# An RWKV-6 mixer with a ternary feed-forward: a fifth product in split form, two moved reductions, and one diagonal copy changed from GpSimd to ScalarE

## The chip, the cores and the metric

One core of a Trainium2 chip runs the program. The metric is device time in microseconds for one launch, the median of several runs. The times name the engines as the profile does: PE is TensorE (its weight loads stand apart as PEld), DVE is VectorE, ACT is ScalarE, POOL is GpSimd, SP is SyncE, which here only issues DMAs.

## What is computed

One layer over x of shape 4 x 2048 x 512 (batch, time, channels), with two residual blocks and a layer normalisation after each:

```python
xx = x_prev - x
mix = tanh((x + xx * time_maa_x) @ maa_w1).reshape(b, t, 5, 32)
mw, mk, mv, mr, mg = einsum('btfe,fec->fbtc', mix, maa_w2)
xk = x + xx * (time_maa_k + mk)          # the same for w, v, r, g
r = xr @ Wr.T;  k = xk @ Wk.T;  v = xv @ Wv.T;  g = silu(xg @ Wg.T)
w = time_decay + tanh(xw @ td_w1) @ td_w2;  decay = exp(-exp(w))
# 16 heads of 32: y_t = r_t (S + u k_t v_t),  S = decay_t S + k_t v_t
y = groupnorm(y) * ln_g + ln_b;  att = (y * g) @ Wo.T
x = layernorm(x + att)
h = gelu(x @ ternary(W_fc).T)
x = layernorm(x + layernorm(h, ln_w, ln_b) @ ternary(W_proj).T)
```

Everything is fp32 at the outside. `mg`, the fifth of the mixing products, is one part of the change.

## The kernel before

The sequence is cut into 32 chunks of 64 steps. A *tile* is one chunk of all four sequences, so 256 columns (`COLS`), with the 512 channels as four groups of 128 partitions. Each engine has a program of its own: `tile(it, first, ffn)` is the attention part of chunk `it`, and between its pieces it calls pieces of the feed-forward of chunk `it - 1` (and a last piece of `it - 2`). Chunks 0 and 1 and the last feed-forward are written out, chunks 2 to 31 are a loop (`over_tiles`). No scheduler is at work: the order on an engine is the order of the code, and engines meet at counting semaphores. PSUM banks go round in rings (`P_SEQ`, `M_SEQ`, `W_SEQ`, `X_SEQ`, `F_SEQ`), each entry with the engine that empties it.

What the change touches, in the order of a tile:

- **The mixing products** (`mix` on PE, L380). ACT takes the tanh of 128 rows for w, k, v, r (`TMA`, L795) and of 32 rows for g (`TMB`, L797). For the first four, the 32 rows of a factor are written four times, one above another, into a 128-row tile `MT[f]`: two copies rounded to the reduced-precision fp32 format (high part, by ACT in `mix_high`, L666), two of what the rounding left (low part, by POOL in `mix_low`, L869). The weights `W2S` are stacked to match (split in setup, L858 and L860), so that one 128-row product of reduced-precision operands gives all four cross terms. The fifth, g, is a plain fp32 product of 32 rows, `W2B` by `TMB`. Each product is four matmuls of 128x256, in two PSUM banks (psX, psY), read by DVE in L1064.
- **The levels.** The recurrence inside a chunk is done by halves: `LEVELS = (2, 4, 8, 16)` and then 32. On each level DVE scales the right halves of the queries (`scale_right`, L1119, with a copy L1107), scales the left halves of the keys (`scale_left`, L1131, and the totals L1132), and takes the level's product from PSUM (L1174). ACT makes three copies of queries for each level (L666), PE the product (L469, for 32 it is L486), followed by a quarter of the down projection of the feed-forward (L642).
- **The folds.** DVE sums GELU values and their squares over the 2048 hidden channels (`add`, L1279 and L1282), and folds four columns of each into one: `fold(p, i)`, L1298, a reduction of 128x512 to 128x128, i = 0 for the values, 1 for the squares. PE multiplies both with ones (`stats`, L632) right after L486. Before the change, for the first half of the tokens, they stand after the levels 4 and 8:

```python
                    dve.wait_ge(w_dve, W.read(it, f"l{n}"))
                    if ffn and n in (4, 8):
                        ffn.fold(0, n // 4 - 1)
                scale(5, 32)
```

- **The diagonal copies.** The 16 x 32 x 32 blocks of the finished matrix `A` are copied onto the diagonal of `AB`, by row groups q = 0 to 3. For the second half (p = 1) ACT makes q = 0 and 1 in `matrices(1)` (L666), then two more copies from PSUM; POOL makes q = 2 and 3 (L909). PE's `from_chunk(1)` (L523) waits for both. ACT then goes on with `squares(0)` (L774), the GELU group `up(1, 0)` (L814, L823, L825), `squares(1)`, and `up(1, 1)`.
- **The end of a tile.** POOL makes the eight low parts, then takes the inverse root of the variance (L876), after which DVE normalises (L1263); in the next tile POOL adds x to the mixed inputs (L883).

Of the kernel before, what the change touches and what calls it, by code (L numbers as in the profile page):

```python
# [104 lines left out]
def rwkv_ffn_kernel(nc, x_ch, x_tok, w_all, w1, w2a, w2b, td1, td2, par, wfc, wpj, ffn_wb, c_f32, c_mask, out,  # L105
                    tiles=TILES):
    with ExitStack() as ctx:
# [39 lines left out]
        TMH = K1[:, 0:COLS]  # L147
# [12 lines left out]
        TMA = sb("TMA", [128, COLS])  # L160
        MTALL = sb("MT", [128, 4, COLS], F32R)
        MT = [MTALL[:, f, :] for f in range(4)]
        TZTM = sb("TZTM", [DECR + MIXR, COLS])
        TZ, TMB = TZTM[0:DECR, :], TZTM[DECR:DECR + MIXR, :]
# [32 lines left out]
        W2RAW = (OUT[:, 0:2, :], X1[:, 0:2, :])  # L197
# [67 lines left out]
        NWEIGHTS = 8 + 4 * 4  # L265
# [15 lines left out]
        def _(sp):  # L281
# [8 lines left out]
            for dst, src in ((W1[:, :, :], w1), (W2B[:, :], w2b), (TD1[:, :, :], td1),  # L290
                             (TD2[:, :], td2), (WALL[:, W_K, :, :], w_all[:, W_K, :, :])):
                sp.dma_start(dst, src).then_inc(weights_in, 16)
            for f in range(4):
                for copy in range(4):
                    sp.dma_start(W2RAW[f // 2][rows(copy), f % 2, :], w2a[rows(f), :]).then_inc(weights_in, 16)
# [35 lines left out]
        def _(pe):  # L331
# [37 lines left out]
            def mix(t, f, name, wait_free):  # L369

                if f < 4:
                    pe.wait_ge(mt_high, 4 * (t + 1) + f + 1)
                    pe.wait_ge(mt_low, 8 * (t + 1) + 2 * f + 2)
                else:
                    pe.wait_ge(tm_ready, M.read(t, "w1b"))
                lhs, rhs = (W2S[:, f, :], MT[f]) if f < 4 else (W2B[:, :], TMB[:, :])
                for g in range(2):
                    wait_free(f"{name}{g}")
                    for c in range(2):
                        mm = pe.matmul(M_BANKS[M.bank(f"{name}{g}")][:, COLS * c:COLS * (c + 1)],  # L380
                                       lhs[:, 128 * (2 * g + c):128 * (2 * g + c + 1)], rhs, start=True, stop=True)
# [282 lines left out]
        def _(act):  # L664
# [3 lines left out]
            def mix_high(t):  # L668

                act.wait_ge(tm_ready, M.read(t, "w1a"))  # L670
                copy(TMH.bitcast(F32R), TMA[:, :]).then_inc(tm_rounded, 1)
                for f in range(4):
# [12 lines left out]
            def tile(it, first, ffn):  # L685
# [21 lines left out]
                act.wait_ge(mt_low, 8 * (it + 1))  # L707
# [46 lines left out]
                def matrices(p):  # L754
# [5 lines left out]
                    for q in range(2 if p else 4):  # L760
# [33 lines left out]
                act.wait_ge(mt_low, 8 * (it + 1))  # L794
# [42 lines left out]
        def _(pool):  # L837
# [24 lines left out]
            def mix_low(t):  # L862

                pool.wait_ge(tm_rounded, t + 2)
                for n in range(8):
                    if n:
                        pool.wait_ge(mt_low, 8 * (t + 1) + n)
                    f = n // 2
                    pool.tensor_tensor(MT[f][rows(1 + 2 * (n % 2)), :], TMA[rows(f), :], TMH[rows(f), :], ALU.subtract).then_inc(mt_low, 1)  # L869
                pool.wait_ge(mt_low, 8 * (t + 1) + 8)  # L870

            pool.wait_ge(w2_split, 4)
# [5 lines left out]
            def tile(it, first, ffn):  # L878
# [93 lines left out]
        def _(dve):  # L972
# [111 lines left out]
            def tile(it, first, ffn):  # L1084
# [80 lines left out]
                for i, n in enumerate(LEVELS):  # L1165
# [52 lines left out]
                dve.wait_ge(ab_rest, 2 * it + 2)  # L1218
# [209 lines left out]
```

## Time and profile before

| | |
|---|---|
| median of 3 runs | 3344.99 us (3342.59 to 3347.0) |
| the profiled execution: its own time, its span | 3343.92 us, 3342.1 us |
| mean granted TensorE clock | 0.993 |
| busy: PE, PEld, DVE, ACT, POOL | 3093.1, 2244.0, 2437.3, 1858.8, 962.3 us |
| chain that ended last, by engine | PE 48%, DVE 31%, issue 11%, ACT 8% |

The table is read from the bottom up: the busy times say how much work each engine has, but the chain says whose work the end waited for. PE is busy 93% of the span and yet only 48% of the chain: in the rest of a tile it has work, or a short wait, while something else is late.

### The profile page before, as it was taken

How to read it: one execution, taken by the hardware profiler on the slowest of the kernel's cores; microseconds unless marked ns; L12 is line 12 of the kernel's file. 1: busy time of each engine (PE TensorE's matmuls, PEld its weight loads, DVE VectorE, ACT ScalarE, POOL GpSimd, SP SyncE). 2: the span in 40 equal slices, each digit the busy share in tenths (PEclk: the TensorE clock that was granted, in tenths of full speed). 3: DMA queues.
4: the chain of work that ended last, by engine and by line, in shares of the span. 5: the costliest groups of instructions: out<-in, count | busy, mean ns of one | idle time of the engine just before them, and what ended most of it. 6: DMA issues, size and time to landing. Idle time of an engine off the chain costs nothing.

```text
span 3342.1 us, 99122 instructions
## 1 busy us (share of the span) xinstructions
PE 3093.1 (93%) x39261; PEld 2244.0 (67%) x39261; DVE 2437.3 (73%) x5172; ACT 1858.8 (56%) x3788; POOL 962.3 (29%) x789
## 2 busy tenths in 40 slices
PE   1899999999999999999999999999999999999997
PEld 0667666767666767666767666767666767666765
DVE  8467787777787777687777687777687677687777
ACT  0445566555566555566655566655566655556654
POOL 4223322223322223322223322223322223322232
PEclk9899999999999999999999999999999999999999
DMA  5000000000000000000000000000000000000000
GB/s 193 14 8 21 15 18 21 18 14 21 15 18 21 18 14 21 18 14 21 18 14 21 21 12 21 18 14 21 21 12 21 18 16 19 21 12 21 18 19 16
DMA packets 22597, 73.04 MB, mean 22 GB/s; under 512 B 3040, under 2 KB 3296, under 8 KB 20544
## 3 DMA queue, kind: packets, MB, share of 16 engines
q1 hardware_dynamic: 22208, 66.76, 5.8%
q8 instruction: 378, 6.19, 0.8%
q14 instruction: 11, 0.09, 0.0%
HBM read 49.97 MB, written 16.78 MB: 20 GB/s over the span
## 4 chain that ended last, share of the span: by engine, by line
PE 48%; DVE 31%; issue 11%; ACT 8%; DVEq 1%; DMA 1%; POOL 0%; ACTq 0%; SPq 0%; POOLq 0%
PE psP L398 11%; PE psF L623 7%; PE psP L430 7%; PE psP L596 5%; DVE ARENA L1131 4%; ACT HHI L823 4%; DVE HLO L1290 4%; DVE ARENA L1174 3%; DVE ARENA L1143 3%; DVE ARENA L1119 3%; DVE SUMS L1282 2%; PE psX L380 2%; ACT GG L814 2%; PE psY L523 2%; PE psY L511 2%
## 5 line engine op out<-in xcount | busy, mean ns | idle before, releaser
L398 PE MATMUL psP<-ARENA,WALL 128*128 128x256 f32 x3072 | 690.9, 382 | 0.2 <-ACT ARENA L697 0.2
L666 ACT ACTIVATE ARENA<-ARENA 32x512 f32<-32x512 f32 (+1 forms) x928 | 537.9, 580 | 252.8 <-DVE ARENA L1119 224.5
L398 PEld LDWEIGHTS psP<-ARENA,WALL 128*128 128x128 f32 x3072 | 574.4, 190 | 83.4 <-issue 11.3
L1290 DVE SCALAR_TENSOR_TENSOR HLO<-GG,FWB,HHI 128x128 f16<-128x128 f32 x1024 | 302.5, 357 | 370.7 <-ACT HHI L823 364.3
L623 PE MATMUL psF<-XHI,WFC 128*128 128x128 f16 x4096 | 488.3, 220 | 2.4 <-DVE ST L1308 2.1
L623 PE MATMUL psF<-XLO,WFC 128*128 128x128 f16 x4096 | 487.1, 220 | 0.0
L883 POOL TENSOR_TENSOR ARENA<-ARENA,XT 128x1024 f32<-128x1024 f32 x128 | 278.4, 2175 | 546.8 <-DVE ARENA L1064 546.8
L623 PEld LDWEIGHTS psF<-XHI,WFC 128*128 128x128 f16 x4096 | 400.7, 99 | 31.5 <-issue 26.2
L623 PEld LDWEIGHTS psF<-XLO,WFC 128*128 128x128 f16 x4096 | 402.1, 98 | 17.6 <-issue 10.3
L642 PE MATMUL psF<-WPJ,HHI 128*128 128x512 f16 x1024 | 390.9, 382 | 3.8 <-ACT GG L814 3.8
L642 PE MATMUL psF<-WPJ,HLO 128*128 128x512 f16 x1024 | 389.4, 380 | 0.0
L823 ACT ACTIVATE HHI<-GG,FWB 128x128 f16<-128x128 f32 x1024 | 327.4, 390 | 25.3
L876 POOL TENSOR_TENSOR FV<-FV,CF 128x1 f32<-128x1 f32 x64 | 43.1, 674 | 1035.7 <-DVE FV L1314 1035.7
L1064 DVE SCALAR_TENSOR_TENSOR ARENA<-psX,PAR,XX 128x256 f32<-128x256 f32 x322 | 140.2, 476 | 235.8 <-PE psX L380 216.3
L814 ACT ACTIVATE GG<-psF 128x512 f32<-128x512 f32 x256 | 152.4, 595 | 280.4 <-PE psP L398 185.3
L869 POOL TENSOR_TENSOR MT<-TMA,ARENA 32x256 fp32r<-32x256 f32 x264 | 258.7, 980 | 95.2 <-ACT ARENA L666 77.1
L596 PE MATMUL psP<-WALL,ARENA 128*128 128x512 f32 x512 | 233.4, 599 | 2.8 <-DVE ARENA L1233 0.2
L430 PE MATMUL psP<-WALL,ARENA 128*128 128x512 f32 x512 | 224.9, 592 | 0.0
L469 PE MATMUL psW<-ARENA 128*32 128x64 f32 x8192 | 142.5, 222 | 66.0 <-ACT ARENA L666 59.2
L469 PEld LDWEIGHTS psW<-ARENA 128*32 128x32 f32 x8192 | 121.9, 111 | 120.8 <-ACT ARENA L666 88.8
L642 PEld LDWEIGHTS psF<-WPJ,HHI 128*128 128x128 f16 x1024 | 100.1, 98 | 126.3 <-issue 16.4
L666 ACT ACTIVATE ARENA<-psP 128x256 f32<-128x256 f32 (+1 forms) x192 | 93.5, 525 | 154.1 <-PE psP L398 154.1
(167 smaller groups left out, 5398.8 us busy)
## 6 DMA issues: line engine op xcount, KB each, us to landing
XT<-x_ch SPq DMA_DIRECT2D x33, 520.0 KB, 3.4
ARENA<-x_tok SPq DMA_DIRECT2D x32, 512.0 KB, 3.8
out<-OUT SPq DMA_DIRECT2D x64, 256.0 KB, 2.1
WALL<-w_all SPq DMA_DIRECT2D x5, 1024.0 KB, 16.7
ARENA<-wfc SPq DMA_DIRECT2D x4, 1024.0 KB, 8.0
ARENA<-wpj SPq DMA_DIRECT2D x3, 1024.0 KB, 14.8
GG<-wpj SPq DMA_DIRECT2D x1, 1024.0 KB, 18.7
OUT<-w2a SPq DMA_DIRECT2D x8, 64.0 KB, 14.8
```

The costliest lines, as they stand in the source:

```text
L398: mm = pe.matmul(psP[:, P.bank(f"{name}{g}"), COLS * c:COLS * (c + 1)], WALL[:, w, k, 128 * (2 * g + c):128 * (2 * g + c + 1)], cc(XF[slot ...
L430: mm = pe.matmul(psP[:, P.bank(f"v{p}"), :], cc(XF[1], k)[:, 128 * p:128 * (p + 1)], WALL[:, W_V, k, :], start=(k == 0), stop=(k == KC - 1))
L469: mm = pe.matmul(psW[BLK * (q % 4):BLK * (q % 4 + 1), W.bank(name), o:o + 64], cc(KM, c)[:, BLK * q:BLK * (q + 1)], RB[RB_SEQ[name]][:, c, ...
L596: mm = pe.matmul(psP[:, P.bank(f"wo{p}"), :], cc(YSB, k)[:, 128 * p:128 * (p + 1)], WALL[:, W_O, k, :], start=(k == 0), stop=(k == KC - 1))
L623: mm = pe.matmul(psF[:, F.bank(name), 128 * m:128 * (m + 1)], WFC[:, k, 128 * (4 * g + m):128 * (4 * g + m + 1)], x[:, p, k, :], start=(k ...
L642: mm = pe.matmul(psF[:, F.bank(f"pj_{p}"), :], h[:, m, :], WPJ[:, m, :], start=(m == 0 and h is HHI), stop=(m == MH - 1 and h is HLO))
L666: return act.activation(o, i, ACT.Copy)
L814: act.activation(GG[:, u % 2, 0, :], psF[:, F.bank(f"fc{g}_{p}"), :], ACT.Gelu).then_inc(f_act, 1)
L823: e = act.activation(HHI[:, k, :], GG[:, u % 2, 0, 128 * m:128 * (m + 1)], ACT.Copy, scale=FWB[:, 0, k:k + 1])
L869: pool.tensor_tensor(MT[f][rows(1 + 2 * (n % 2)), :], TMA[rows(f), :], TMH[rows(f), :], ALU.subtract).then_inc(mt_low, 1)
L883: pool.tensor_tensor(v, v, xcur, ALU.add).then_inc(xf_ready, 1)
L1290: e = dve.scalar_tensor_tensor(out=HLO[:, k, :], in0=GG[:, u % 2, 0, 128 * m:128 * (m + 1)], scalar=FWB[:, 0, k:k + 1], in1=HHI[:, k, :], ...
```

## The change

It has three parts.

1. `mg` is made as the other four: a fifth slot in `W2S` and in `MT`, two more rounded copies on ACT per tile and one of `TMB` itself (`TMBH`), two more low parts on POOL. `TMA`, `TMH`, `TMB` and `TMBH` now lie in the four quarters of `K1`. In setup, four DMAs bring the weights of g into `V` in place of one, and POOL has one more cast and one more subtraction.
2. `fold(0, 0)` stands after level 2, and `fold(0, 1)` between `scale_right(5, 32)` and `scale_left(5, 32)`.
3. For p = 1, ACT copies q = 0, 1, 2 and POOL only q = 3.

```diff
             def mix(t, f, name, wait_free):
-                if f < 4:
-                    pe.wait_ge(mt_high, 4 * (t + 1) + f + 1)
-                    pe.wait_ge(mt_low, 8 * (t + 1) + 2 * f + 2)
-                else:
-                    pe.wait_ge(tm_ready, M.read(t, "w1b"))
-                lhs, rhs = (W2S[:, f, :], MT[f]) if f < 4 else (W2B[:, :], TMB[:, :])
+                pe.wait_ge(mt_high, 5 * (t + 1) + f + 1)
+                pe.wait_ge(mt_low, 10 * (t + 1) + 2 * f + 2)
+                lhs, rhs = W2S[:, f, :], MT[f]
...
             def mix_high(t):
-                act.wait_ge(tm_ready, M.read(t, "w1a"))
+                act.wait_ge(tm_ready, M.read(t, "w1b"))
                 copy(TMH.bitcast(F32R), TMA[:, :]).then_inc(tm_rounded, 1)
-                for f in range(4):
-                    copy(MT[f][rows(0), :], TMA[rows(f), :])
-                    copy(MT[f][rows(2), :], TMA[rows(f), :]).then_inc(mt_high, 1)
+                copy(TMBH.bitcast(F32R), TMB[:, :]).then_inc(tm_rounded, 1)
+                for f in range(5):
+                    src = TMA[rows(f), :] if f < 4 else TMB
+                    copy(MT[f][rows(0), :], src)
+                    copy(MT[f][rows(2), :], src).then_inc(mt_high, 1)
...
-                    for q in range(2 if p else 4):
+                    for q in range(3 if p else 4):
...
             def mix_low(t):
-                pool.wait_ge(tm_rounded, t + 2)
-                for n in range(8):
+                pool.wait_ge(tm_rounded, 2 * t + 4)
+                for n in range(10):
...
-                for q in range(2, 4):
-                    if q == 3:
-                        pool.wait_ge(ab_rest, 2 * it + 1)
-                    r = slice(BLK * q, BLK * (q + 1))
-                    block = A[r, 512:1024].rearrange("p (h t) -> p h t", h=HEADS)
-                    pool.tensor_tensor(AB[r, :, BLK * q:BLK * (q + 1)], block, ONES[r, 0:BLK].unsqueeze(1).broadcast_to([BLK, HEADS, BLK]), ALU.mult).then_inc(ab_rest, 1)
-                pool.wait_ge(ab_rest, 2 * it + 2)
+                r = slice(BLK * 3, BLK * 4)
+                pool.tensor_tensor(AB[r, :, BLK * 3:BLK * 4], A[r, 512:1024].rearrange("p (h t) -> p h t", h=HEADS),
+                                   ONES[r, 0:BLK].unsqueeze(1).broadcast_to([BLK, HEADS, BLK]), ALU.mult).then_inc(ab_rest, 1)
+                pool.wait_ge(ab_rest, it + 1)
...
                     dve.wait_ge(w_dve, W.read(it, f"l{n}"))
-                    if ffn and n in (4, 8):
-                        ffn.fold(0, n // 4 - 1)
-                scale(5, 32)
+                    if ffn and n == 2:
+                        ffn.fold(0, 0)
+                scale_right(5, 32)
+                if ffn:
+                    ffn.fold(0, 1)
+                scale_left(5, 32)
```

The order of instructions, at three places. DVE in the levels of a tile before the change; GR<-SUMS is a fold, ARENA<-CM,psW the taking of a level's product (128x128x4 is level 4, 128x64x8 level 8):

```order
L1174 COPY_PREDICATED ARENA<-CM,psW 128x128x4
L1298 TENSOR_REDUCE GR<-SUMS 128x128
L1119 TENSOR_TENSOR ARENA<-ARENA,TOT 128x64x8
L1107 COPY ARENA<-ARENA 32x4x128
L1131 TENSOR_TENSOR ARENA<-ARENA,TOT 128x64x8
L1132 TENSOR_TENSOR TOT<-TOT 128x64
L975 MEMSET PAUSE 1x1
L1174 COPY_PREDICATED ARENA<-CM,psW 128x64x8
L1298 TENSOR_REDUCE GR<-SUMS 128x128
L1119 TENSOR_TENSOR ARENA<-ARENA,TOT 128x32x16
```

DVE in the changed kernel, from the taking of level 2's product on:

```order
L1169 COPY_PREDICATED ARENA<-CM,psW 128x256x2
L1296 TENSOR_REDUCE GR<-SUMS 128x128
L1114 TENSOR_TENSOR ARENA<-ARENA,TOT 128x128x4
L1102 COPY ARENA<-ARENA 32x4x128
L1126 TENSOR_TENSOR ARENA<-ARENA,TOT 128x128x4
```

The first fold has moved one level forward. DVE in the changed kernel, from the taking of level 16's product on:

```order
L1169 COPY_PREDICATED ARENA<-CM,psW 128x32x16
L1114 TENSOR_TENSOR ARENA<-ARENA,TOT 128x16x32
L1296 TENSOR_REDUCE GR<-SUMS 128x128
L1126 TENSOR_TENSOR ARENA<-ARENA,TOT 128x16x32
L1127 TENSOR_TENSOR TOT<-TOT 128x16
```

The second fold has moved behind the level 16 and stands between the two scalings of level 32; no fold is left between levels 4 and 16. ACT from the copies out of psX (the transposed keys) to the GELU group after, before the change:

```order
L666 ACTIVATE ARENA<-psX 128x512 x2
L666 ACTIVATE ARENA<-ARENA 32x16x32 x2
L666 ACTIVATE ARENA<-psW 32x16x32 x2
L774 ACTIVATE ARENA<-ARENA 128x4x128
L814 ACTIVATE GG<-psF 128x512
```

and in the changed kernel:

```order
L661 ACTIVATE ARENA<-psX 128x512 x2
L661 ACTIVATE ARENA<-ARENA 32x16x32 x3
L661 ACTIVATE ARENA<-psW 32x16x32 x2
L771 ACTIVATE ARENA<-ARENA 128x4x128
L811 ACTIVATE GG<-psF 128x512
```

One more diagonal copy stands ahead of the copies from psW, which PE waits for, and ahead of the GELU group.

## Rows read from the trace of the kernel before

**Rows 1.** The page: busy times, and the chain by engine.
```profile
PE 3093.1 (93%) x39261; PEld 2244.0 (67%) x39261; DVE 2437.3 (73%) x5172; ACT 1858.8 (56%) x3788; POOL 962.3 (29%) x789
PE 48%; DVE 31%; issue 11%; ACT 8%; DVEq 1%; DMA 1%; POOL 0%; ACTq 0%; SPq 0%; POOLq 0%
```

**Rows 2.** By tile: count, duration min/median/max ns, first and last start us.
```profile
L797 ACT ACTIVATE TZTM<-psY x32: 371/371/373, 179.7 to 3280.4; 32x256 f32<-32x256 f32 x32
L869 POOL TENSOR_TENSOR MT<-TMA,ARENA x264: 713/726/1947, 91.1 to 3288.1; 32x256 fp32r<-32x256 f32 x132
```

**Rows 3.** The chain of waits, 1700 to 1810: start us, us, what.
```profile
1713.27 1.05 PE psX L380 x4
...
1715.19 3.67 PE psP L398 x16
...
1719.03 0.61 ACT GG L814
...
1804.06 0.29 PE psX L380 x2
...
1804.58 5.58 PE psP L430 x13
```

**Rows 4.** Timeline of DVE: start us, us, what, [idle before <-releaser].
```profile
1744.78 0.69 DVE L1174 COPY_PREDICATED ARENA<-CM,psW 128x512 f32<-128x512 uint32 x1
...
1745.51 1.08 DVE L1298 TENSOR_REDUCE GR<-SUMS 128x128 f32<-128x512 f32 x1
1746.52 0.67 DVE L1119 TENSOR_TENSOR ARENA<-ARENA,TOT 128x512 f32<-128x512 f32 x1
...
1748.53 0.72 DVE L1174 COPY_PREDICATED ARENA<-CM,psW 128x512 f32<-128x512 uint32 x1
1749.44 0.69 DVE L1119 TENSOR_TENSOR ARENA<-ARENA,TOT 128x512 f32<-128x512 f32 x1 [0.19 <-DVE ARENA L1174]
1751.32 0.69 DVE L1131 TENSOR_TENSOR ARENA<-ARENA,TOT 128x512 f32<-128x512 f32 x1 [1.19 <-PE psW L486]
...
1792.74 1.83 DVE L1263 TENSOR_SCALAR X<-X,MV,RSTD 128x512 f32<-128x512 f32 x2
```

**Rows 5.** Timeline of PE.
```profile
1745.50 1.10 PE L469 MATMUL psW<-ARENA 128*32 128x64 f32 x64 [1.05 <-ACT ARENA L666]
...
1748.05 0.38 PE L642 MATMUL psF<-WPJ,HLO 128*128 128x512 f16 x1
1749.33 1.94 PE L486 MATMUL psW<-ARENA 128*32 128x128 f32 x32 [0.90 <-DVE ARENA L1174]
...
1759.15 1.08 PE L523 MATMUL psY<-ARENA,V 128*32 128x128 f32 x32 [0.85 <-issue]
```

**Rows 6.** Timeline of ACT.
```profile
1743.54 1.91 ACT L666 ACTIVATE ARENA<-ARENA 32x512 f32<-32x512 f32 x3 [2.08 <-DVE ARENA L1119]
...
1755.44 1.27 ACT L666 ACTIVATE ARENA<-ARENA 32x512 f32<-32x512 f32 x2 [0.44 <-PE psY L523]
1756.74 1.19 ACT L666 ACTIVATE ARENA<-psW 32x512 f32<-32x512 f32 x2
...
1761.02 0.62 ACT L774 ACTIVATE ARENA<-ARENA 128x512 f32<-128x512 f32 x1
1762.16 0.60 ACT L814 ACTIVATE GG<-psF 128x512 f32<-128x512 f32 x1 [0.52 <-PE psF L623]
```

**Rows 7.** Timeline of POOL: setup, then a tile.
```profile
91.07 6.30 POOL L869 TENSOR_TENSOR MT<-TMA,ARENA 32x256 fp32r<-32x256 f32 x8 [8.03 <-ACT ARENA L666]
...
1755.58 3.47 POOL L909 TENSOR_TENSOR ARENA<-ARENA,CF 32x512 f32<-32x512 f32 x2 [1.86 <-PE psY L523]
...
1779.75 8.51 POOL L869 TENSOR_TENSOR MT<-TMA,ARENA 32x256 fp32r<-32x256 f32 x8 [2.10 <-ACT ARENA L666]
1789.56 0.70 POOL L876 TENSOR_TENSOR RSTD<-RSTD,CF 128x2 f32<-128x2 f32 x1 [1.30 <-DVE RSTD L1255]
1791.65 2.18 POOL L883 TENSOR_TENSOR ARENA<-ARENA,XT 128x1024 f32<-128x1024 f32 x1 [1.39 <-DVE ARENA L1064]
```

More of the change, by code:

```diff
@@ L146, in rwkv_ffn_kernel @@
         K1 = ARENA1[:, 7168:8192]
-        TMH = K1[:, 0:COLS]
+        TMA, TMH = K1[:, 0:COLS], K1[:, COLS:2 * COLS]
+        TMB, TMBH = K1[0:MIXR, 2 * COLS:3 * COLS], K1[0:MIXR, 3 * COLS:4 * COLS]
         KT = ARENA1[:, 7168:8192].rearrange("p (q n) -> p q n", q=PAIRS)
@@ L159, in rwkv_ffn_kernel @@
         XX = sb("XX", [128, KC * B, CH])
[L160 to L164, printed above, removed]
+        MTALL = sb("MT", [128, 5, COLS], F32R)
+        MT = [MTALL[:, f, :] for f in range(5)]
+        TZ = sb("TZ", [DECR, COLS])[:, :]
         TOT = {1: D}
@@ L264, in rwkv_ffn_kernel @@
         NPL = len(LEVELS) + 2
[L265 removed]
+        NWEIGHTS = 7 + 5 * 4
         POOL_PARTS = (2, 5, 7)
@@ L289, in _ @@
             sp.dma_start(WALL[:, W_V, :, :], w_all[:, W_V, :, :]).then_inc(values_in, 16)
-            for dst, src in ((W1[:, :, :], w1), (W2B[:, :], w2b), (TD1[:, :, :], td1),
+            for dst, src in ((W1[:, :, :], w1), (TD1[:, :, :], td1),
                              (TD2[:, :], td2), (WALL[:, W_K, :, :], w_all[:, W_K, :, :])):
                 sp.dma_start(dst, src).then_inc(weights_in, 16)
-            for f in range(4):
+            for f in range(5):
                 for copy in range(4):
-                    sp.dma_start(W2RAW[f // 2][rows(copy), f % 2, :], w2a[rows(f), :]).then_inc(weights_in, 16)
+                    sp.dma_start(W2RAW[f // 2][rows(copy), f % 2, :], w2a[rows(f), :] if f < 4 else w2b).then_inc(weights_in, 16)
             for w in (W_R, W_G, W_O):
@@ L668, in mix_high @@
             def mix_high(t):
-                act.wait_ge(tm_ready, M.read(t, "w1a"))
+                act.wait_ge(tm_ready, M.read(t, "w1b"))
                 copy(TMH.bitcast(F32R), TMA[:, :]).then_inc(tm_rounded, 1)
-                for f in range(4):
-                    copy(MT[f][rows(0), :], TMA[rows(f), :])
-                    copy(MT[f][rows(2), :], TMA[rows(f), :]).then_inc(mt_high, 1)
+                copy(TMBH.bitcast(F32R), TMB[:, :]).then_inc(tm_rounded, 1)
+                for f in range(5):
+                    src = TMA[rows(f), :] if f < 4 else TMB
+                    copy(MT[f][rows(0), :], src)
+                    copy(MT[f][rows(2), :], src).then_inc(mt_high, 1)
             act.wait_ge(su_dve, 6)
@@ L853, in _ @@
             pool.wait_ge(weights_in, 16 * NWEIGHTS)
-            for i in range(2):
+            for i in range(3):
                 if i:
-                    pool.wait_ge(w2_split, 2)
-                w = W2S[:, 2 * i:2 * (i + 1), :]
+                    pool.wait_ge(w2_split, 2 * i)
+                w = W2S[:, 2 * i:min(2 * i + 2, 5), :]
                 pool.tensor_copy(w, W2RAW[i]).then_inc(w2_split, 1)
@@ L862, in mix_low @@
             def mix_low(t):
-                pool.wait_ge(tm_rounded, t + 2)
-                for n in range(8):
+                pool.wait_ge(tm_rounded, 2 * t + 4)
+                for n in range(10):
                     if n:
-                        pool.wait_ge(mt_low, 8 * (t + 1) + n)
+                        pool.wait_ge(mt_low, 10 * (t + 1) + n)
                     f = n // 2
-                    pool.tensor_tensor(MT[f][rows(1 + 2 * (n % 2)), :], TMA[rows(f), :], TMH[rows(f), :], ALU.subtract).then_inc(mt_low, 1)
-                pool.wait_ge(mt_low, 8 * (t + 1) + 8)
-            pool.wait_ge(w2_split, 4)
+                    whole, high = (TMA[rows(f), :], TMH[rows(f), :]) if f < 4 else (TMB, TMBH)
+                    pool.tensor_tensor(MT[f][rows(1 + 2 * (n % 2)), :], whole, high, ALU.subtract).then_inc(mt_low, 1)
+                pool.wait_ge(mt_low, 10 * (t + 1) + 10)
+            pool.wait_ge(w2_split, 6)
             mix_low(-1)
```

19 lines of the change are left out of this document (9 added, 10 removed).

## The prediction

> **What bounds the kernel now.** I read the page first. PE is busy 93% of the span, but makes only 48% of the chain that ended last, and DVE 31% [rows 1]. So no engine bounds it alone: inside each tile the lead changes hands, and a saving counts only where its engine leads. The second view, by tile, gives the period: the tanh of L797 starts 32 times, from 179.7 to 3280.4 us [rows 2], so 31 periods take 3100.7 us, 100.02 us each. Setup and end take the other 7% of the span and are hardly touched, so the question is what one period loses. The third view, the chain in order of time over one period in the middle, says who leads; the timelines of the engines say how much slack the others have. Four stretches of it matter:
>
> - 1711 to 1719: PE leads. The product of g stands on the chain, and ACT's GELU (L814) waits for the first r product behind it [rows 3].
> - 1721 to 1749: DVE leads, through the levels. The folds lie in it: the fold of level 8 starts as soon as the product is taken and the next scaling right behind it [rows 4].
> - 1749 to 1762: PE leads, with one wait of 0.85 us before L523 [rows 5]. The view calls it "issue", but by the code PE waits there for POOL's diagonal copies, and those end at 1755.58 + 3.47 = 1759.05 [rows 7].
> - from 1762.16 on ACT leads with the GELU groups. It had been idle for only 0.52 us before that [rows 6].
>
> **The g product.** Removed: four fp32 matmuls, from 1713.27 to the start of the r product at 1715.19, so 1.92 us. Added: four matmuls in the split form. The v product of the same shape and form takes from 1804.06 to 1804.58, so 0.52 us [rows 3]. Difference 1.40 us per tile, all of it on the chain, since ACT waits for PE behind it and DVE's levels wait for ACT; everything up to the levels moves with it. 32 tiles: **-44.8 us**. The new waits of that product (ten low parts, five high ones) end at about 1790 us of the tile, 20 us before PE comes to it: nothing. Bounds: 0 if the new form ran like the old, 1.92 if it were free; the row of the same form is nearest, so 1.40. The Trainium skill says (FP8 and Floating Point Precision, TensorE Precision Notes) that a true fp32 product takes four passes through the array. By that estimate three quarters of 1.92 go, 1.44, and the sum would be 1.3 us lower; no row shows passes.
>
> Its price elsewhere: ACT makes one more rounded copy ahead and two behind, at a place where PE leads with the output projection: nothing. POOL's first piece waits for one copy more, about 0.4 us. The eight pieces take 6.30 us in setup and 8.51 us in the tile [rows 7], with pieces between 0.71 and 1.95 us [rows 2]: in the tile, pieces stand and wait beside DVE, the first among them, so a later start of 0.4 us is mostly swallowed. Two more pieces, 0.80 us each (6.30 / 8), end at 1788.26 + 1.6 = 1789.86. Behind them in POOL's queue stands the root, which waited 1.30 us for DVE anyway [rows 7]; it comes 0.3 us late, and DVE uses it at 1792.74 only [rows 4], 2.2 us after its new end. The next addition, at 1791.65 [rows 7], finds POOL free by 1.1 us. So nothing per tile, but in the last tile, where no other work is there, the root is on the path: +0.3 us. If this cover were gone, 1.6 us per tile would show. In setup POOL is idle for 8.03 us before its low parts [rows 7]; one more cast and subtraction fit into that, as they are half the size of those before. Three more small DMAs land long before POOL asks. Setup: 0.
>
> **The folds.** Before, from the end of the taken product of level 8, 1744.78 + 0.69 = 1745.47, to the next scaling at 1746.52 are 1.05 us. Without a fold, after level 16, it is 1749.44 - 1749.25 = 0.19 us [rows 4]. So a fold costs the chain of levels 0.86 us. `fold(0, 0)` pays this after level 2 instead of level 4: no change at the start of level 8. `fold(0, 1)` leaves the levels: -0.86 us, if nobody else is then late. ACT's three copies for level 16's product end at 1743.54 + 1.91 = 1745.45 [rows 6], and the scaling that waits for them would start at 1745.66: 0.2 us to spare. PE's product at 1745.50 ends at 1746.60, and DVE's left scaling, which waits for it, would come at about 1746.8: also 0.2. Then L486: before it PE waited 0.90 us for DVE, with the down projection done at 1748.43 [rows 5]. Now DVE ends at 1748.39 and PE is late next, by nothing: -0.86 us is about all there was. In its new place the fold starts behind the right scaling and fills the 1.19 us in which DVE waited for L486 [rows 4]; it needs 1.05, so 0.1 us remain. The sums that it makes are needed by PE only after L486. 31 tiles have a feed-forward in them: **-26.7 us**. Bounds: 0 to 0.90 us per tile; if both slacks are 0.2 us less than I think, 0.5 is left.
>
> **The diagonal copy.** POOL's 3.47 us shrink to one copy, some 1.3 to 2.1 us, and end by 1757.7. ACT's two copies of 1.27 us become three, +0.635, so the copies from psW, which PE needs too, end at 1757.93 + 0.635 = 1758.57 [rows 6]. PE starts L523 at about 1758.6 instead of 1759.15: 0.55 us early. But behind it ACT becomes the late one: its work up to the GELU group at 1762.16 is contiguous but for 0.52 us, and 0.635 more is added. The chain from there on loses 0.115 us per tile: **+3.6 us**. What PE gains is spent waiting. Bounds: -0.55 if PE still led, +0.635 if there were no slack at all; the row with the 0.52 is the direct one.
>
> **Sum.** -44.8 - 26.7 + 3.6 + 0.3 = -67.6 us. The profiled execution took 3343.92, so 3276.3; it lies 1.07 under the median of the runs, so I forecast **3277 us**, 2.0% less. About 0.2%, 7 us, is what a measurement of this kernel can tell from no change. The forecast's own range is 3270 to 3290.
>
> **The rivals.**
>
> - *The fold's gain is lost* (0.09). Level 8's product on PE now comes 0.9 us later relative to the down projection, since its queries are scaled behind the first fold; if that pushed the next level's product, or ACT's copies were 0.9 us late, DVE would wait where it now folds. Against it: the two slacks above are positive. Then 3277 + 26.7 = 3304.
> - *PE keeps the lead after L523* (0.08), because ACT has more slack than one period shows. Then the copy gains 0.55 instead of losing 0.115: 31 x 0.665 = 20.6, and 3256.
> - *The g product does not get faster* (0.04), for instance by weight loads that do not hide behind such short matmuls. But the v, r, k and w products are the same instructions. 3277 + 44.8 = 3322.
> - *POOL and DVE hold each other: slower* (0.03). Pieces beside DVE took up to 1.95 us [rows 2]. If all ten of a tile did, with gaps of 0.08, they would end 20.3 us after 1779.75, at 1800.0; the root and the addition behind them may start no later than 1790.95. The excess of 9.1 us, less the 2.15 saved, would add 6.95 us to 31 tiles: 3345 + 215 = 3560. It decides from an end at 1793.1 on, that is at 1.33 us per piece with its gap, where the eight now take 1.06. Against it: all eight together lose 2.21 us to setup's 6.30 [rows 7], and where the two new ones fall, after 1788.3, DVE has by the code small statistics and reads from PSUM. The Trainium skill (SBUF — State Buffer, SBUF: two separate sides) has VectorE and GpSimd take one shared port pair as an exclusive lock: whoever starts first keeps it for the whole instruction, the other blocks. The 6.30 against 8.51 us agrees with it.
> - *Nothing measurable comes out* (0.02): gains in the first part of a tile are given back at its end, where DVE normalises. The chain has no such wait in it.
>
> The remaining 0.74 is the forecast, with small misses of its terms. The range of 3262 to 3302 takes in half of each of the two likely rivals: the fold term nearly gone, or two thirds of the diagonal gain. Faster 0.95, same 0.02, slower 0.03.
>
> **What would show it.** Right: the period falls to about 97.9 us; the g product takes 0.5 us on PE; between the taking of levels 4 and 8 and the next scaling stand 0.2 us, not 1.05; PE's wait before L486 goes from 0.90 to under 0.1 us, and DVE's before the last left scaling from 1.19 to about 0.1; ACT's idle time of 0.52 before the second GELU group is gone, and PE's 0.85 before L523 shrinks to 0.3. Wrong: a new wait of DVE or ACT inside the levels; a root of the variance that DVE waits for; ten low parts that take over 12 us; ACT still idle before that GELU.

## The result, and the profile after

| | before | after |
|---|---|---|
| median of the runs | 3345.03 us (3342.59 to 3347.0) | 3308.34 us (3307.6 to 3310.75) |
| ratio | | 0.9893, 95% interval 0.9881 to 0.9905 |
| span of the profiled execution | 3342.1 us | 3305.7 us |
| mean granted TensorE clock | 0.993 | 0.982 |
| mean period of a tile | 100.02 us [rows 2] | 99.0 us |

The change saves 36.7 us where 68 were forecast: the direction was right, and the time lies 6 us above the range. One number of this table had no place in the forecast, the clock. Its mean fell by 0.011.

The busy times and the chain by engine, from the page of the changed kernel (to be compared with [rows 1]):

```profile
PE 3080.0 (93%) x39133; PEld 2229.9 (67%) x39133; DVE 2449.2 (74%) x5172; ACT 1913.6 (58%) x3919; POOL 933.9 (28%) x825
PE 48%; DVE 27%; ACT 13%; issue 10%; DVEq 1%; DMA 1%; ACTq 0%; POOL 0%; SPq 0%; POOLq 0%
```

DVE's share of the chain fell from 31% to 27% and ACT's rose from 8% to 13%. The fold that left the levels is under 1% of the span and explains little of that; the rest is lead that went from one engine to another. But PE's stayed at 48%, though 1.4 us of its work left the chain in every tile. That asked for a look at PE itself. First the new g product (L375, four matmuls) and the first r product behind it, then the same engine around levels 8 and 32 (columns: start us, us, what, idle before and its releaser; rows of L637, the down projection, partly left out):

```profile
1695.57 0.48 PE L375 MATMUL psX<-MT,W2S 128*128 128x256 f32 x2
1695.89 0.40 PE L375 MATMUL psY<-MT,W2S 128*128 128x256 f32 x2
1696.13 7.07 PE L393 MATMUL psP<-ARENA,WALL 128*128 128x256 f32 x32
...
1721.13 0.38 PE L637 MATMUL psF<-WPJ,HLO 128*128 128x512 f16 x1
1723.59 1.93 PE L464 MATMUL psW<-ARENA 128*32 128x64 f32 x64 [2.08 <-ACT ARENA L661]
1725.45 0.61 PE L637 MATMUL psF<-WPJ,HHI 128*128 128x512 f16 x1
...
1727.75 0.38 PE L637 MATMUL psF<-WPJ,HLO 128*128 128x512 f16 x1
1728.06 1.10 PE L464 MATMUL psW<-ARENA 128*32 128x64 f32 x64
...
1730.92 1.94 PE L481 MATMUL psW<-ARENA 128*32 128x128 f32 x32
```

The g product is as forecast: from 1695.57 to the r product at 1696.13, 0.56 us. The move of the folds also did its part at the end: PE no longer waits before level 32 (L481), where it had waited 0.90 us [rows 5]. But the same 64 matmuls of L464 take 1.93 us at level 8 and 1.10 us at level 16, and a matmul of the down projection takes 0.61 and 0.38 us. The windows view over level 8 of four tiles (columns: stretch, us, busy time and count of PE, weight loads, DVE, ACT, POOL, then the granted clock, DMA share, GB/s):

```profile
1622.00:1627.00 5.00, 2.91 (x69) 1.97 (x68) 4.13 (x10) 3.13 (x5) 0.00 (x0) 0.77 0.01 3
1722.00:1727.00 5.00, 3.41 (x68) 2.27 (x69) 4.16 (x11) 3.39 (x6) 0.00 (x0) 0.66 0.02 3
1820.00:1825.00 5.00, 2.88 (x69) 1.97 (x67) 4.16 (x9) 3.15 (x6) 0.00 (x0) 0.76 0.02 3
1919.00:1924.00 5.00, 2.89 (x74) 1.59 (x73) 4.63 (x11) 2.90 (x5) 0.00 (x0) 1.00 0.01 3
```

In three of these four tiles TensorE's granted clock fell from full speed (2.4 GHz) to half of it (1.2 GHz), and it came back 3.41 us later, by the trace's record of the clock. It does not fall in the middle of PE's wait, but when the wait is over or a little after it. Here is the tile of the timeline above (the wait, the stretch behind it, the time after), then another tile in which the product of level 8, from 2316.60, still ran at full speed and the down projection behind it did not:

```profile
1721.50:1723.55 2.05, 0.01 (x1) 0.00 (x0) 1.94 (x6) 1.88 (x3) 0.00 (x0) 1.00 0.00 0
1723.65:1727.00 3.35, 3.35 (x68) 2.21 (x69) 2.58 (x7) 1.88 (x3) 0.00 (x0) 0.50 0.02 5
1727.10:1729.00 1.90, 1.90 (x69) 1.23 (x67) 1.15 (x3) 0.86 (x2) 0.00 (x0) 1.00 0.00 0
```

```profile
2316.60 1.10 PE L464 MATMUL psW<-ARENA 128*32 128x64 f32 x64 [2.10 <-ACT ARENA L661]
```

```profile
2314.60:2316.55 1.95, 0.00 (x0) 0.00 (x0) 1.84 (x6) 1.88 (x3) 0.00 (x0) 1.00 0.00 0
2316.60:2317.55 0.95, 0.95 (x64) 0.93 (x64) 0.76 (x2) 0.00 (x0) 0.00 (x0) 1.00 0.00 0
2317.60:2320.95 3.35, 3.35 (x16) 1.04 (x8) 3.02 (x8) 2.16 (x4) 0.00 (x0) 0.50 0.02 5
```

Of the 31 tiles with a feed-forward beside them, 23 have such a fall, a *low stretch* of 3.41 us. It begins between 0.03 us before and 0.97 us after the start of level 8's product, 51 to 52 us after the tanh into `TZ` (L684, L687 before), from which all places in a tile are counted below; the 64 matmuls of level 8 take 1.10 to 1.93 us accordingly. Before the change the clock never fell between 200 and 3150 us. Who pays for it is on DVE's timeline, at levels 8 and 16:

```profile
1724.64 0.42 DVE L1102 COPY ARENA<-ARENA 32x512 f32<-32x512 f32 x1
1725.57 0.69 DVE L1126 TENSOR_TENSOR ARENA<-ARENA,TOT 128x512 f32<-128x512 f32 x1 [0.50 <-PE psW L464]
...
1728.05 0.42 DVE L1102 COPY ARENA<-ARENA 32x512 f32<-32x512 f32 x1
1729.23 0.69 DVE L1126 TENSOR_TENSOR ARENA<-ARENA,TOT 128x512 f32<-128x512 f32 x1 [0.75 <-PE psW L464]
```

DVE leads through the levels when the clock is high. Here it waits 0.50 and 0.75 us for PE's slowed products, and the chain of waits goes over PE from 1723.59 to 1732.89.

What a fall costs can be read inside this one kernel, since the tiles with and without one run the same instructions, and PE waits 2.05 to 2.13 us before level 8 in all of them. From the end of the low parts of unit (0,1) to the keys' transposes behind the levels it is 30.29 us in the tiles with a fall (30.25 to 30.33) and 29.00 in those without (28.68 to 29.07); these are 22 and 8 tiles, the last one left out. So a fall costs 1.29 us, and 23 of them 29.7 us of the time.

A second, smaller loss lies ahead of the levels. POOL, then DVE, at the low parts of the second GELU unit, after and then before the change:

```profile
1699.95 2.50 POOL L931 TENSOR_TENSOR OUT<-X,BSUM 128x512 f32<-128x512 f32 x2
```

```profile
1701.95 1.44 DVE L1288 SCALAR_TENSOR_TENSOR HLO<-GG,FWB,HHI 128x128 f16<-128x128 f32 x4 [4.21 <-ACT HHI L820]
```

```profile
1718.31 2.49 POOL L936 TENSOR_TENSOR OUT<-X,BSUM 128x512 f32<-128x512 f32 x2
...
1721.05 1.14 DVE L1290 SCALAR_TENSOR_TENSOR HLO<-GG,FWB,HHI 128x128 f16<-128x128 f32 x4 [4.95 <-ACT HHI L823]
```

Before, POOL's two bias additions ended at 1720.80, a quarter of a microsecond ahead of DVE's four low parts. Now the low parts start 1.56 us earlier in the tile but POOL's additions only 0.82, so that DVE starts at 1701.95 while POOL works until 1702.45; the four take 1.44 us, not 1.14.

To see what each stage lost I took the same events in 25 tiles of the loop from the trace of each kernel and averaged their distance from the tanh into `TZ` (us; the runs named e... follow below):

| event | before | after | e1 | e2 | e3 | e4 |
|---|---|---|---|---|---|---|
| GELU of unit (0,1) starts | 28.98 | 27.43 | 27.49 | 27.45 | 27.49 | 29.01 |
| its low parts end on DVE | 32.14 | 30.89 | 30.95 | 30.91 | 30.95 | 32.17 |
| keys' transposes on PE, behind the levels | 62.06 | 60.88 | 60.02 | 59.95 | 60.87 | 61.20 |
| GELU of unit (1,1) | 72.15 | 71.00 | 70.15 | 70.07 | 70.98 | 71.30 |
| GELU of unit (1,2) | 76.52 | 75.48 | 74.85 | 74.37 | 75.50 | 75.65 |
| next tile | 100.09 | 99.00 | 98.36 | 97.79 | 98.98 | 99.15 |

### The profile page after: what moved, and what is told of

Its sections match the earlier page's. It is cut to its first block, busy times and chain, and to the rows that moved or that the text cites. A ratio compares the mean times of both kernels' runs of the same rounds, so it can differ in the third digit from the quotient of the medians.

```text
span 3305.7 us, 98915 instructions
## 1 busy us (share of the span) xinstructions
PE 3080.0 (93%) x39133; PEld 2229.9 (67%) x39133; DVE 2449.2 (74%) x5172; ACT 1913.6 (58%) x3919; POOL 933.9 (28%) x825
## 4 chain that ended last, share of the span: by engine, by line
PE 48%; DVE 27%; ACT 13%; issue 10%; DVEq 1%; DMA 1%; ACTq 0%; POOL 0%; SPq 0%; POOLq 0%
PE psP L393 10%; PE psP L425 7%; PE psF L637 5%; PE psP L591 5%; ACT HHI L820 4%; PE psF L618 4%; DVE HLO L1288 4%; ACT ARENA L661 3%; DVE ARENA L1138 3%; ACT GG L811 2%; DVE SUMS L1280 2%; DVE ARENA L1126 2%; PE psW L464 2%; PE psW L481 2%; DVE ARENA L1169 2%
## 5 line engine op out<-in xcount | busy, mean ns | idle before, releaser
L661 ACT ACTIVATE ARENA<-ARENA 32x512 f32<-32x512 f32 (+3 forms) x1026 | 581.1, 569 | 263.9 <-DVE ARENA L1114 202.1
L637 PE MATMUL psF<-WPJ,HHI 128*128 128x512 f16 x1024 | 405.7, 396 | 4.7 <-ACT GG L811 4.7
L637 PE MATMUL psF<-WPJ,HLO 128*128 128x512 f16 x1024 | 402.3, 393 | 0.0
L867 POOL TENSOR_TENSOR MT<-ARENA 32x256 fp32r<-32x256 f32 x330 | 297.4, 901 | 107.0 <-ACT ARENA L661 83.7
L464 PE MATMUL psW<-ARENA 128*32 128x64 f32 x8192 | 154.4, 232 | 71.2 <-ACT ARENA L661 63.4
L464 PEld LDWEIGHTS psW<-ARENA 128*32 128x32 f32 x8192 | 131.9, 117 | 125.4 <-ACT ARENA L661 82.1
L637 PEld LDWEIGHTS psF<-WPJ,HHI 128*128 128x128 f16 x1024 | 103.2, 101 | 138.0 <-issue 37.1
```

The lines of the kernel that those rows point to most:

```text
L464: mm = pe.matmul(psW[BLK * (q % 4):BLK * (q % 4 + 1), W.bank(name), o:o + 64], cc(KM, c)[:, BLK * q:BLK * (q + 1)], RB[RB_SEQ[name]][:, c, ...
L637: mm = pe.matmul(psF[:, F.bank(f"pj_{p}"), :], h[:, m, :], WPJ[:, m, :], start=(m == 0 and h is HHI), stop=(m == MH - 1 and h is HLO))
L661: return act.activation(o, i, ACT.Copy)
L867: pool.tensor_tensor(MT[f][rows(1 + 2 * (n % 2)), :], whole, high, ALU.subtract).then_inc(mt_low, 1)
```

## The experiments

The theory before the first run: the fold now behind level 2 and the earlier end of PE's work lengthen PE's wait before level 8 from 0.90 to 2.08 us, the clock falls in it, and that costs about 1 us a tile. The rivals: the clock is a bystander, and the folds (or the new product) lose their gain by their place; or ACT's extra copies do. The ratios are to the kernel before, whose median beside these runs was 3343.66 (e1 to e4), 3343.94 (e5, e6, e7, e9) and 3345.94 us (e10, e12, e13).

### e1: the first fold back behind level 4

```diff
-                    if ffn and n == 2:
+                    if ffn and n == 4:
                         ffn.fold(0, 0)
```

> The changed kernel with the first fold back after level 4; the second stays between the scalings of level 32. Theory CLOCK (the first fold after level 2 lengthens PE's wait before level 8 from 0.90 to 2.08 us, and in most tiles the granted clock halves for 3.4 us after it; that costs 1.0 us per tile): PE's waits are about 0.9 us again, the mean granted clock is 0.99, and the time is 3277 us, which the prediction had. Rival SCALARE (ACT's extra copies, the diagonal one above all, cost more than they were priced at): no change, 3308 us. Rival LATE PRODUCT (PE's product of level 8, with the down projection behind it, comes late for DVE by its place alone, whatever the clock): 3277 to 3285 us too; the run with the filled wait tells this one from CLOCK.

Measured: 3284.15 us (3280.41 to 3289.18), ratio 0.9816 (0.98 to 0.9832). PE's wait before level 8 is 1.22 us and no tile of the loop has a low stretch:

```profile
1713.12 1.10 PE L464 MATMUL psW<-ARENA 128*32 128x64 f32 x64 [1.22 <-ACT ARENA L661]
```

Moving one instruction of DVE by one level gives back 24 us. ACT's extra copies are all still there, so they are not what lost it. This alone doesn't separate the clock from another effect of the fold's place.

### e2: the wait before level 8 filled

The fold stays behind level 2, and PE multiplies weights with each other while it would wait, into the bank that level 8 overwrites:

```diff
                     W.wait_free(pe, it, name, first)
+                    if ffn and i == 2:
+                        for _ in range(8):
+                            pe.matmul(psW[:, W.bank(name), :], WPJ[:, 0, 0:128], WPJ[:, 0, :], start=True, stop=True, skip_group_check=True)
                     pe.wait_ge(k_scaled, NPL * it + i + 1)
```

> The changed kernel, and in PE's wait before level 8 eight matmuls of constant weights by constant weights (128x512 fp16, about 1.7 us), into the bank that the product then overwrites: the output is the same. PE has 1.7 us more work per tile and no time to itself. CLOCK: the clock stays high, 0.99, the products of level 8 take 1.10 us again and not 1.93, and the time falls from 3308 to 3277 to 3285 us. LATE PRODUCT: no fall, 3308 us or some more. SCALARE: 3308 us.

Measured: 3272.15 us (3272.03 to 3273.49), ratio 0.9785 (0.9769 to 0.9801), clock 0.993, no low stretch in the loop, mean period 97.79 us. The timeline of PE, with the filling:

```profile
1703.78 1.89 PE L460 MATMUL psW<-WPJ 128*128 128x512 f16 x8
1706.02 1.10 PE L467 MATMUL psW<-ARENA 128*32 128x64 f32 x64 [0.35 <-ACT ARENA L664]
```

DVE's program is that of the change, and PE has more to do; the kernel is 36 us faster. The table says where: of the 1.21 us a tile, 0.93 are gained up to the keys' transposes (59.95 against 60.88), in the levels, 0.18 in the stretch with the product of the state (GELU (1,1) to (1,2)) and 0.10 behind it. The 0.93, 29 us in 31 tiles, are what the falls cost; the clock is the cause there and no bystander. The other 0.28 us are something else that the eight matmuls changed (below).

### e3 and e4: the parts apart

e3 is the change with both folds and the diagonal copies as before, so the new product alone; e4 is the kernel before with the folds of the change alone.

> Of the change only the g product in split form; folds and diagonal copies as before. The prediction's term alone: 3345 - 44.8 = 3300 us, with PE's waits in the levels as before and the clock at 0.99. If ACT and POOL pay for the extra pieces (SCALARE), 3305 to 3320 us.

> The kernel before with only the two folds moved. CLOCK: the same long wait of PE before level 8, clock 0.98, so 26.7 us are gained and some 31 lost: 3345 to 3350 us. LATE PRODUCT: the same. SCALARE: the folds are innocent, 3345 - 26.7 = 3318 us.

Measured: e3 3311.1 us (3309.76 to 3311.99), ratio 0.99 (0.9884 to 0.9917); e4 3315.53 us (3314.63 to 3315.82), ratio 0.9913 (0.9896 to 0.9929). Neither has a low stretch in the loop. The folds alone give 28.1 us, where the forecast's term was 26.7. The product alone gives 32.6 us and not 44.8. Added, the two make 60.7 us; the whole change gives 36.7.

For e4 my expectation under the clock's theory was wrong: I took the fold's place to be enough for the fall. PE's wait before level 8 is 1.80 us there, between the 0.90 before and the 2.08 after:

```profile
1729.78 1.10 PE L469 MATMUL psW<-ARENA 128*32 128x64 f32 x64 [1.80 <-ACT ARENA L666]
```

As medians over the tiles, the wait is 0.91 us before, 1.22 with the product alone (e3), 1.78 with the folds alone (e4) and 2.10 with both. So the fold adds 0.87 us to the wait and the product 0.31, and of these four kernels only the one with both shows falls in the loop. The loss needs two parts of the change, and neither part shows it alone.

### e5 and e6: the diagonal copy

e5 is the kernel before with the diagonal copies of the change alone (by its code it is ScalarE that makes three of them; the expectation names VectorE); e6 is e1 with them as before.

> The kernel before with the change's third part alone: VectorE makes three of the diagonal copies, GpSimd one. The forecast priced it at +0.115 us a tile, 3348 us (3345 to 3352). The milestones of the runs so far (keys' transposes to the GELU of unit (1,1): 10.09 us before, 10.13 after, 10.12 with the copy as before) say about nothing: 3344 to 3346 us.

> The change with the first fold behind level 4 (3284 us, high clock) and two diagonal copies back on GpSimd, as before. If the third part of the change costs its 0.115 us a tile within the rest of the change: 3280 to 3281 us. If it costs nothing: 3283 to 3286 us. The stalls of TensorE in the state product that this placing of the fold showed (0.3 us a tile) come or go with where the instructions lie, and may move it by up to 10 us downwards; where the state product is free of them, that is seen in the trace.

Measured: e5 3337.51 us (3335.92 to 3339.68), ratio 0.9982 (0.9973 to 0.9992); e6 3286.54 us (3282.39 to 3288.74) beside e1's 3284.15. Both say that the third part costs nothing; if anything it gains. In the means from the keys' transposes to the GELU of unit (1,1), the stretch in which it lies, 10.09 us became 10.10 in e5. e5's 6 us come later in the tile: 0.06 us of each period in the stretch with the product of the state (4.31 for 4.37), the rest behind it. What makes them is not shown.

### e7: the first fold behind level 8

```diff
-                    if ffn and n == 2:
+                    if ffn and n == 8:
                         ffn.fold(0, 0)
```

> The change with the first fold moved from behind level 2 to behind level 8 of the fifth product's tile. TensorE's wait before level 8 then is about 1.2 us as with the fold behind level 4, and its wait before level 16 grows from 1.07 by a fold's 0.9 to about 1.95 us. If the clock falls on the length of TensorE's wait alone (2.08 us in the change, 1.80 us did not do it in the folds alone), 1.95 us lies between the two: a fall in some tiles or none, and then behind level 8, the low matmuls being level 16's. None: 3272 to 3287 us. In most tiles: 3300 to 3312 us. If instead the place (what TensorE did before the wait) decides, no fall whatever the wait: 3272 to 3287 us.

Measured: 3280.71 us (3279.04 to 3284.56), ratio 0.9816 (0.98 to 0.9833), no low stretch. This was meant as a wait of 1.95 us in another place, and it was no such thing; my expectation of the wait was wrong. PE waits 1.22 us before level 8, 0.14 before level 16 and 1.01 before level 32, since a fold delays the level two behind it, and the wait that e1 has before level 16 exists only because its fold stands behind level 4. So the run says no more of the clock than e1 did; it shows that behind level 8 the fold is at least as good as behind level 4 (3280.71 and 3284.15 us, with ranges that overlap).

### e12 and e13: a longer wait without the product, a shorter one with it

e12 is e4 (without the new product) with a longer wait: DVE clears a spare tile of 128x384 elements behind the first fold. e13 is e2 with one matmul in the wait, not eight.

```diff
                     if ffn and n == 2:
                         ffn.fold(0, 0)
+                        dve.memset(SPARE[:, :], 0.0)
```

```diff
-                        for _ in range(8):
+                        for _ in range(1):
```

> The kernel before with the folds of the change alone (3315.5 us, TensorE's wait before level 8 is 1.80 us, no fall of the clock), and VectorE also clears a spare tile of 128x384 elements behind the first fold, 0.2 to 0.45 us that serve nothing. TensorE's wait grows to 2.0 to 2.25 us, as long as in the whole change (2.08 us), without the new product of the fifth mixing. If the length of that wait alone makes the clock fall: low stretches of 3.4 us behind it in most tiles, 0.9 to 1.3 us a tile for them beside the clearing's own 0.2 to 0.45 us, 3345 to 3368 us. If the new product has a part in it (less work of TensorE earlier in the tile): no low stretches, the clearing's own time alone, 3321 to 3330 us.

> The change with one idle matmul in TensorE's wait before level 8 where the filled wait had eight. It is over 0.2 us into the wait, so some 1.8 us of it are left empty, as in the folds alone, where the clock stayed high. If the length of the empty stretch decides: no low stretch or a few, 3272 to 3280 us. If the wait has to be filled nearly whole, as the eight did: low stretches as in the change, 3300 to 3310 us.

Measured: e12 3338.77 us (3336.96 to 3339.57), ratio 0.9978 (0.9968 to 0.9987); e13 3292.74 us (3289.49 to 3295.41), ratio 0.984 (0.9824 to 0.9857). PE at level 8, e12 and then e13:

```profile
1742.21 1.10 PE L470 MATMUL psW<-ARENA 128*32 128x64 f32 x64 [2.13 <-ACT ARENA L667]
```

```profile
1713.07 0.38 PE L460 MATMUL psW<-WPJ 128*128 128x512 f16 x1
1715.31 1.10 PE L467 MATMUL psW<-ARENA 128*32 128x64 f32 x64 [1.87 <-ACT ARENA L664]
```

Both fell between my two cases. Side by side, over the 31 tiles with a feed-forward:

| kernel | PE's wait before level 8, median, us | new product | tiles with a fall of the clock there |
|---|---|---|---|
| before | 0.91 | no | 0 |
| e3 | 1.22 | yes | 0 |
| e1 | 1.21 | yes | 0 |
| e4 | 1.78 | no | 0 |
| e13 | 1.87, one matmul ahead of it | yes | 5 |
| after | 2.10 | yes | 23 |
| e12 | 2.14 | no | 7 |
| e2 | 0.37, eight matmuls ahead of it | yes | 0 |

e12 makes the clock fall without the new product, by the length of the wait; that part of the theory holds. Length isn't all: 2.14 us gave 7 falls and 2.10 us with the new product 23. In e12 and e13 the falls also begin later, 0.96 to 1.47 us after the wait's end, where the change has up to 0.97. What else decides no run here separates.

The price of a fall is the same in all three kernels. The stretch from the low parts of (0,1) to the keys' transposes is 30.68 us with a fall and 29.39 without in e12, and 30.31 and 29.03 in e13: 1.29 and 1.28 us. So e12's 23 us over e4 are about 9 for seven falls and 11 for the clearing (29.39 for 29.03 us in each tile). The five falls of e13 are only 6 of its 20.6 us over e2; 0.2 us a tile more lie in the stretch with the product of the state, and the rest is not accounted for.

### e9 and e10: POOL's second bias addition put off, and the best version

e9 is e2, and POOL makes the second bias addition only when DVE has added the sums of unit (1,1), a time at which DVE is idle; until then POOL has nothing else to do.

```diff
-                    for p in range(PAIRS):
-                        pool.wait_ge(x1_ready, PAIRS * j + p + 1)
-                        pool.tensor_tensor(OUT[:, p, :], X1[:, p, :], BSUM[:, :], ALU.add).then_inc(x1_biased, 1)
+                    pool.wait_ge(x1_ready, PAIRS * j + 1)
+                    pool.tensor_tensor(OUT[:, 0, :], X1[:, 0, :], BSUM[:, :], ALU.add).then_inc(x1_biased, 1)
+
+                def bias_second():
+                    pool.wait_ge(x1_ready, PAIRS * j + 2)
+                    pool.wait_ge(sums_added, 3 * (PAIRS * j + 1) + 1)
+                    pool.wait_ge(x1_biased, PAIRS * j + 1)
+                    pool.tensor_tensor(OUT[:, 1, :], X1[:, 1, :], BSUM[:, :], ALU.add).then_inc(x1_biased, 1)
```

`bias_second` is called behind the root of `normed`. e10 is e9 with the first fold behind level 4.

> The change with TensorE's wait before level 8 filled (3272 us) and, besides, GpSimd's bias addition for the second half of the tokens put off until VectorE has added the sums of unit (1,1), so that it no longer runs beside VectorE's first low parts of unit (0,1). If that pair is what lengthens those four low parts from 1.14 to 1.44 us and costs 0.30 us a tile: 0.30 x 31 = 9 us less, 3260 to 3265 us. If the lengthening is hidden or comes from something else: 3271 to 3274 us. If the addition now delays GpSimd's own chain (its product with z, the low parts): over 3275 us.

> The kernel with the wait filled and GpSimd's second bias addition put off (3262 us), with the first fold behind level 4 and not behind level 2. The stalls of TensorE in the state product, 0.3 to 1.0 us without a wait for a semaphore, came with this placing of the fold in two kernels (3284 and 3287 us) and were not there with the fill. If the placing of the fold makes them: a period 0.3 to 0.5 us longer, 3271 to 3278 us. If they hang on how TensorE's instructions lie and come in, which the fill has shifted: gone here as well, 3260 to 3265 us.

Measured: e9 3262.23 us (3261.16 to 3262.89), ratio 0.9756 (0.974 to 0.9772); e10 3262.34 us (3260.83 to 3262.85), ratio 0.9747 (0.973 to 0.9763). POOL, then DVE, in e9:

```profile
1678.74 1.27 POOL L933 TENSOR_TENSOR OUT<-X,BSUM 128x512 f32<-128x512 f32 x1
```

```profile
1680.73 1.14 DVE L1302 SCALAR_TENSOR_TENSOR HLO<-GG,FWB,HHI 128x128 f16<-128x128 f32 x4 [4.21 <-ACT HHI L823]
```

The low parts are back at 1.14 us, and the kernel is 9.9 us faster than e2, 0.32 us for each of 31 tiles. So DVE's 0.30 us came from POOL's addition beside it, and they lay on the path. In the changed kernel the first of the four took 652 ns and the others 337 to 339, by the view of the tile:

```profile
L1288 DVE SCALAR_TENSOR_TENSOR HLO<-GG,FWB,HHI x4: 337/339/652, 1702.0 to 1703.1; 128x128 f16<-128x128 f32 x4
```

It started at 1701.95 and ended at 1702.60, just behind the end of POOL's addition at 1702.45, and the others ran as ever. The Trainium skill (SBUF — State Buffer, SBUF: two separate sides) says that such a pair doesn't share: the later one is blocked until the first is through. An estimate by that rule is a loss of what is left of POOL's instruction when DVE comes, here 0.50 us, and an end of DVE's first instruction at about 1702.79. The trace agrees in form (one instruction long, three normal) but not in size: the loss is 0.31 us and the end 1702.60.

e9 and e10 are the fastest versions that were run, 2.4% below the kernel before and 1.4% below the change.

One more thing was to be seen in e10: in some kernels PE stalls in the product of the state (L546) with no semaphore to wait for, in e1 for 0.17 to 0.81 us in every tile. The chain of waits of e1 there (start us, us, what):

```profile
1733.89 0.03 PE psX L546 x2
1733.92 0.81 issue
1734.73 0.23 PE psY L546 x4
```

By the table, the stretch from GELU (1,1) to GELU (1,2) takes 4.37 us before, 4.48 after, 4.70 in e1, 4.52 in e3 and 4.30 in e2. In e10 it is 4.31, with e1's place of the fold, and in e13 with its single extra matmul 4.49. So the fold's place alone doesn't make the stalls: with eight more matmuls ahead of them in PE's program they are gone, with one they are not. Whether that is the way in which PE's instructions come in, or something else, nothing here shows; it stays open.

## Why the prediction was wrong, point by point

- **g product, 1.92 to 0.52 us:** right on PE (0.56 us). With a slightly earlier start and a shorter r product, the GELU behind it comes 1.55 us earlier in the table, where 1.40 was forecast.
- **"Everything up to the levels moves with it":** wrong by 0.30 us a tile. The step looked at PE, ACT and DVE and not at what POOL does beside DVE at that moment. The gap between POOL's end and DVE's start was 0.25 us before; DVE's work then moved by 1.56 us and POOL's by 0.82, so that they overlap by 0.50. e9 showed it; it explains most of what the product alone (e3, -32.6 us) lacks to -44.8. I had POOL and DVE holding each other on record as a rival, but put it at the low parts of the next mixing, where it cost the path nothing: the ten take 9.80 us, and the root behind them still waits 0.16 us for DVE:

```profile
1761.61 9.80 POOL L867 TENSOR_TENSOR MT<-ARENA 32x256 fp32r<-32x256 f32 x10 [2.41 <-ACT ARENA L661]
1771.57 0.70 POOL L874 TENSOR_TENSOR RSTD<-RSTD,CF 128x2 f32<-128x2 f32 x1 [0.16 <-DVE RSTD L1253]
```

- **Folds, -0.86 us:** right without the falls of the clock; in the changed kernel the term came to +0.07 us, as the next point says. From the low parts of (0,1) to the keys' transposes 29.92 us became 29.04 in e2, and the folds alone gave 28.1 us for 26.7. PE's wait before level 32 went from 0.90 to nothing, and DVE's behind it to 0.26 us, forecast 0.1:

```profile
1731.59 1.05 DVE L1296 TENSOR_REDUCE GR<-SUMS 128x128 f32<-128x512 f32 x1
1732.91 0.69 DVE L1126 TENSOR_TENSOR ARENA<-ARENA,TOT 128x512 f32<-128x512 f32 x1 [0.26 <-PE psW L481]
```

- **"fold(0, 0) pays this after level 2 instead of level 4: no change at the start of level 8":** this is the step that failed. DVE starts the scalings of level 8 at the same time, yes, but PE's product of level 8 now starts 5.08 us after DVE begins to take level 2's (1718.51 to 1723.59) where it was 4.20 (1737.31 to 1741.51), and PE's two waits, of 0.90 us before level 8 (the row below, of before) and 1.05 us before level 16 [rows 5], became one of 2.08 us before level 8. The prediction put the longer wait at nothing: I costed a wait by who is late at its end and never asked what it does to PE itself. What the runs showed in its place is a fall of TensorE's clock behind that wait in 23 of 31 tiles, at 1.29 us each. The stretch from the low parts to the keys' transposes, which should have shrunk from 29.92 to 29.06 us, is 29.99 in the changed kernel: +0.95 us a tile against e2, and the whole gain of the folds gone. The rival that the fold's gain is lost (3304 us) had the place and nearly the size, and named the late product of level 8, but its mechanism, DVE waiting because the queries or ACT's copies come late, isn't what happened: with the clock held up (e2), the same order of DVE loses nothing.
```profile
1741.51 1.10 PE L469 MATMUL psW<-ARENA 128*32 128x64 f32 x64 [0.90 <-ACT ARENA L666]
```

- **Diagonal copy, +0.115:** the stretch grew by 0.03 us, and e5 and e6 find no cost. PE's wait before the second from_chunk product fell from 0.85 to 0.42 us (forecast 0.3), and ACT's idle time before the GELU is gone, as forecast:

```profile
1740.27 1.08 PE L518 MATMUL psY<-ARENA,V 128*32 128x128 f32 x32 [0.42 <-ACT ARENA L661]
```

```profile
1740.15 0.63 ACT L771 ACTIVATE ARENA<-ARENA 128x512 f32<-128x512 f32 x1
1740.81 0.60 ACT L811 ACTIVATE GG<-psF 128x512 f32<-128x512 f32 x1
```

- **The sum.** Deviations per tile: product -0.15, low parts beside POOL +0.30, folds -0.02, clock +0.95, diagonal copy -0.09, stalls of the state product +0.11, the rest -0.05: together +1.05 us, times 31 makes 33 us. The forecast of 3277 plus that is 3310; 3308.3 was measured. Without the 29.7 us of the falls it would have been 3279: the rest of the sum held because its other misses nearly cancel, which is partly luck.

## What to carry to other kernels

A wait that costs nobody anything can still cost the clock: when an edit merges two short waits of TensorE into a longer one, look at the granted clock of that stretch and of the work just behind it, compare tiles with a fall and tiles without, and fill the wait with idle matmuls or split it again before giving up the edit. And when a stretch of work moves by a microsecond, list what GpSimd does beside VectorE at its new place; a pair that just missed each other before is a term of the sum. Parts that are each measured alone don't show a loss that needs both.

## What the runs showed of the hardware

- TensorE's clock fell to 1.2 GHz behind single waits of about 2 us, at their end or up to 1.5 us later, and stayed there for 3.41 us each time: in 23 of 31 tiles at 2.10 us, in 7 at 2.14 us in another kernel, in none at 1.78. Each fall cost 1.29 us. The 64 matmuls of level 8 took up to 1.93 us for 1.10. I had not expected this in a kernel whose PE is busy 93% of the span. The Trainium skill (TensorE: Matmul & The Clock Gate, HAM oscillation) tells of a kernel whose TensorE waits for data in every step of its loop and pays for the fall each time; the trace agrees in kind, with at most one fall a tile, at one and the same place.
- Eight matmuls that compute nothing made the kernel 36 us faster, about 29 of them by the clock. One made it 16 us faster and left 5 falls.
- A scalar_tensor_tensor of DVE that began 0.50 us before the end of a tensor_tensor of POOL's took 0.65 us for 0.34.
- PE stood for 0.17 to 0.81 us in every tile of e1, without a semaphore that the profile shows, in a stretch of many short matmuls. With the eight matmuls in a place some 20 us ahead (e2) the longest such gap was 0.08 us; the cause wasn't settled.
